# A fused decoder layer: query-phase out-products later, the state's wait for one turned half, another value order, and silu written back into its bank

## The reference, cut to what matters

```
qkv = silu(x @ qkv_w.T)                 # 2 x 512 tokens, 32 heads of 128; q, k, v per head
per block: scores = (q @ k.T) * decay;  intra = scores @ v
           inter  = (q * q_decay) @ state;  state = state * block_decay + (k * k_decay).T @ v
out  = intra + inter
out  = rms_norm(out) * norm_w
out  = sigmoid(x @ gate_w.T) * out
x    = layernorm(x + out @ out_w.T)
```

## Time and profile before

| | |
|---|---|
| runs, median (lowest to highest) | 1945.45 us (1941.33 to 1946.73), three runs |
| profiled execution | 1941.43 us, span 1939.6 us |
| TensorE busy | 93% of the span |
| VectorE / ScalarE / GpSimd busy | 71% / 50% / 33% |
| mean granted TensorE clock | 0.976 |

### The profile page before, as it was taken

One profiled execution on the slowest core, in us unless ns is written; L12 is line 12 of the kernel. 1 busy time (PEld: TensorE's weight loads), 2 busy tenths in 40 slices (PEclk: granted clock), 3 DMA queues, 4 the chain that ended last, 5 costly groups with the idle time before them and its releaser, 6 DMA issues.

```text
span 1939.6 us, 27666 instructions
## 1 busy us (share of the span) xinstructions
PE 1808.5 (93%) x9865; PEld 896.1 (46%) x9865; DVE 1383.3 (71%) x1867; ACT 975.0 (50%) x1432; POOL 641.9 (33%) x506
## 2 busy tenths in 40 slices
PE   6999999999999999999999999999999999999887
PEld 4454535444454534444453544444453544575432
DVE  8677677676777767777766767667676766758877
ACT  5554545544464544545454544545444454544674
POOL 2352323324342333334232332434233332301333
PEclk9999999999999999999999999999999999999998
DMA  4213214231422223041321313131221413233332
GB/s 180 67 66 105 86 66 103 67 103 44 129 62 95 74 87 104 31 133 50 115 76 37 101 55 84 42 102 57 66 71 55 104 46 87 80 100 118 109 88 88
DMA packets 158118, 161.53 MB, mean 83 GB/s; under 512 B 99872, under 2 KB 127904, under 8 KB 157600
## 3 DMA queue, kind: packets, MB, share of 16 engines
q1 hardware_dynamic: 146528, 147.09, 25.6%
q0 software_dynamic: 2560, 8.39, 1.3%
q10 hardware_dynamic: 8896, 4.28, 0.8%
HBM read 123.56 MB, written 12.58 MB: 70 GB/s over the span
## 4 chain that ended last, share of the span: by engine, by line
PE 54%; DVE 17%; issue 16%; ACT 9%; POOL 3%; DMA 1%; ACTq 0%; DVEq 0%; POOLq 0%; SPq 0%
PE bank L1386 13%; PE bank L1387 13%; PE bank L1388 13%; DVE w_pair L1740 4%; PE bank L1359 4%; PE bank L1473 3%; PE bank L1475 3%; PE bank L1474 2%; DVE acc L1908 2%; POOL ssq L2052 1%; ACT sig L1636 1%; DVE gated_split L1740 1%; ACT k_units L1643 1%; ACT w_pair L1601 1%; PE bank L1537 1%
## 5 line engine op out<-in xcount | busy, mean ns | idle before, releaser
L1386 PE MATMUL bank<-x_blocks,w_pair 128*128 128x512 f16 (+1 forms) x1820 | 687.9, 378 | 23.8 <-DVE bank L1788 12.1
L1387 PE MATMUL bank<-x_blocks,w_pair 128*128 128x512 f16 (+1 forms) x1820 | 686.6, 377 | 0.0
L1388 PE MATMUL bank<-x_blocks,w_pair 128*128 128x512 f16 (+1 forms) x1820 | 685.5, 377 | 0.0
L2026 POOL TENSOR_TENSOR sums_pair<-raw_pair 128x512 f32<-128x512 f32 x63 | 93.5, 1485 | 647.8 <-DVE w_pair L1740 453.5
L1386 PEld LDWEIGHTS bank<-x_blocks,w_pair 128*128 128x128 f16 x1820 | 180.1, 99 | 237.4 <-DVE bank L1788 20.1
L1388 PEld LDWEIGHTS bank<-x_blocks,w_pair 128*128 128x128 f16 x1820 | 179.9, 99 | 208.8 <-issue 10.4
L1387 PEld LDWEIGHTS bank<-x_blocks,w_pair 128*128 128x128 f16 x1820 | 180.2, 99 | 195.4 <-issue 12.0
L1908 DVE TENSOR_TENSOR acc<-acc,bank 128x512 f32<-128x512 f32 x320 | 212.0, 681 | 43.6 <-PE bank L1475 41.9
L1473 PE MATMUL bank<-w_vo,gated_split 128*128 128x512 f16 x392 | 150.8, 385 | 57.2 <-issue 54.5
L1636 ACT ACTIVATE sig<-bank 128x512 f32<-128x512 f32 x145 | 86.4, 596 | 227.0 <-PE bank L1388 192.1
L1740 DVE SCALAR_TENSOR_TENSOR w_pair<-raw_pair,w_pair 128x1024 f16<-128x1024 f32 x126 | 170.2, 1370 | 14.0 <-ACT w_pair L1601 13.9
(11 more groups left out here) (208 smaller groups left out, 2792.4 us busy)
## 6 DMA issues: line engine op xcount, KB each, us to landing
raw_pair<-w_qk SPq DMA_DIRECT2D x32, 1024.0 KB, 5.5
raw_pair<-w_gate SPq DMA_DIRECT2D x16, 1024.0 KB, 4.9
raw_pair<-w_out SPq DMA_DIRECT2D x16, 1024.0 KB, 4.9
raw_pair<-w_vt SPq DMA_DIRECT2D x15, 1024.0 KB, 4.9
raw_pair<-ctx_in SPq DMA_DIRECT2D x8, 1024.0 KB, 4.9
decay_sb<-rates SPq DMA_DIRECT2D x60, 128.0 KB, 4.5
acc<-x_t SPq DMA_DIRECT2D x4, 1024.0 KB, 11.5
ctx<-raw_pair SPq DMA_DIRECT2D x8, 512.0 KB, 3.2
```

What stands on the lines that cost most here:

```text
L1386: pe.matmul(out, w_hi, x_hi, start=unmet and k == 0, stop=False, skip_group_check=halves or not fresh)
L1387: pe.matmul(out, w_hi, x_lo, start=False, stop=False, skip_group_check=halves or not fresh)
L1388: mm = pe.matmul(out, w_lo, x_hi, start=False, stop=k == QT - 1, skip_group_check=halves or not fresh)
L2026: pool.tensor_tensor(s3, a11, a21, ALU.add)
```

## The change

Four edits. In the query pair the out stages 0 to 2, and the splits and sums that feed them, move one or two products later, and weight splits 0 and 1 of the next pair move from product 6 to products 5 and 4. The value pair's order becomes 1, 7, 6, 2, 4, 5, 3. The state product waits for the turned even unit alone (`v_first`), not for both of its head's units. And silu writes its result back to where it read it (bank or `p7_copy`), so the `sig` tiles are no longer needed for it; the place is released when the low half is written (for k's units 0 and 2, when the decay multiplication has read it) instead of after the silu.

```diff
 def qk_out(self, which, r):
     done, place, sign = self.result(r)
-    gi, silu, lo = self.silu(...)
-    self.release(place, silu)
-    if which == "k" and r % 2 == 0:
-        self.kd[r // 2] = gi, lo
+    silu, lo = self.silu(...)
+    if which == "k" and r % 2 == 0:
+        self.kd[r // 2] = place, silu
+    else:
+        self.release(place, lo)
...
 def decay_keys(self, g):
-    gi, lo = self.kd[g]
-    self.add("k_decay", g=g, gi=gi, lo=lo, rate=self.rate_ready[g])
+    place, silu = self.kd[g]
+    gi = self.sig_at % 2
+    self.sig_at += 1
+    self.add("k_decay", g=g, gi=gi, place=place, silu=silu, sig_free=self.sig_free[gi], rate=self.rate_ready[g])
     rate = self.rate_free[g] = self.sig_free[gi] = self.tick("k_rate")
+    self.release(place, rate)
...
 # state: what it waits for
-    v=[t for b in range(B) for t in self.v_done[b][g]]
+    v=self.v_first[g]
...
 # kv_out, v_out and end_v
-    self.release(place, silu)
+    self.release(place, lo)
...
+    self.v_first = [[self.v_turned[2]], [self.v_turned[0]]]
...
 # the query pair's slots, order (1, 2, 7, 6, 5, 4, 3) as before
     "p1": [attend(3), gated(3)] + gate_rest,
-    "p2": sums(S2) + stages(0) + [lambda: plan.qk_out("q", 0)] + units(3) + split_sum(S2) + sums(S1),
-    "p7": stages(1) + split_sum(S1) + sums(S4) + split_sum(S4),
-    "p6": stages(2) + [part(0), part(1)],
+    "p2": sums(S2) + [lambda: plan.qk_out("q", 0)] + units(3),
+    "p7": split_sum(S2) + sums(S1) + stages(0) + sums(S4),
+    "p6": split_sum(S1) + stages(1) + split_sum(S4),
+    "p5": stages(2) + [part(0)],
+    "p4": [part(1)],
     "p3": stages(3) + [part(2)],
...
 # the value pair
-}, (1, 7, 6, 4, 2, 5, 3))
+}, (1, 7, 6, 2, 4, 5, 3))
...
 # ScalarE, silu
-    until(act, sem, st["sig_free"])
-    act.activation(c.sig32[st["gi"]][:, :], c.placed(st["place"]), ACT.Silu, ...)
-    src = c.sig32[st["gi"]][:, :]
+    src = c.placed(st["place"])
+    act.activation(src, src, ACT.Silu, ...)
...
 # VectorE, silu's low half and the decay
-    src = c.sig32[st["gi"]][:, :]
+    src = c.placed(st["place"])
...
-    dve.wait_ge(sem["qkv_lo"], st["lo"][1])
+    dve.wait_ge(sem["silu"], st["silu"][1])
+    until(dve, sem, st["sig_free"])
     until(dve, sem, st["rate"])
-    dve.tensor_tensor(k, k, c.rate(st["g"], B), ALU.mult)
+    dve.tensor_tensor(k, src, c.rate(st["g"], B), ALU.mult)
```

More of the change, by code:

```diff
@@ L329, in silu @@
     def silu(self, done, place, sign, dst, dst_free):
[L331 to L333 removed]
+        st = self.add("silu", done=done, place=place, sign=sign, silu=self.tick("silu"),
                       dst=dst, free=dst_free if isinstance(dst_free, list) else [dst_free], slot=self.late_slot,
                       hi=self.tick("qkv_hi"))
[L336 to L337 removed]
+        return st["silu"], self.tick("qkv_lo")
     def qk_out(self, which, r):
         done, place, sign = self.result(r)
[L341 to L343 removed]
+        silu, lo = self.silu(done, place, sign, (which, r), [self.qk_free, self.g_split] if which == "k" else
+                             [self.qk_free, self.q_read])
         if which == "k" and r % 2 == 0:
[L345 removed]
+            self.kd[r // 2] = place, silu
+        else:
+            self.release(place, lo)
         for b in range(B):
@@ L366, in state @@
         i, bank, free = self.main_ring.take()
-        self.add("state", g=g, bank=bank, free=free, turned=self.k_turned[g], v=[t for b in range(B) for t in self.v_done[b][g]],
+        self.add("state", g=g, bank=bank, free=free, turned=self.k_turned[g], v=self.v_first[g],
                  mm=self.tick("state_mm"), hi=self.tick("st_hi"))
@@ L374, in kv_out @@
         done, place, sign = self.result(r)
-        _, silu, lo = self.silu(done, place, sign, ("kv", b, r), [self.qk_free, self.g_split, self.late_units_free])
-        self.release(place, silu)
+        silu, lo = self.silu(done, place, sign, ("kv", b, r), [self.qk_free, self.g_split, self.late_units_free])
+        self.release(place, lo)
         self.qk_done[("k", r // 2, b)] = lo
@@ L385, in v_out @@
         done, place, sign = self.result(r)
-        _, silu, lo = self.silu(done, place, sign, ("v_unit", r), self.s_free if r == 2 else self.vo_free)
-        self.release(place, silu)
+        silu, lo = self.silu(done, place, sign, ("v_unit", r), self.s_free if r == 2 else self.vo_free)
+        self.release(place, lo)
         self.add("v_turn", r=r, ready=lo, free=max(self.v_hl_free))
@@ L420, in end_v @@
         bank = v["banks"][half]
-        _, silu, done = self.silu(v["mm"][half], bank, 1.0, ("v", v["b"], half), self.v_hl_free[v["b"]])
+        silu, done = self.silu(v["mm"][half], bank, 1.0, ("v", v["b"], half), self.v_hl_free[v["b"]])
         self.v_done[v["b"]] = [[done]] * GH
-        self.main_ring.give(bank, silu)
+        self.v_first = [[done]] * GH
+        self.main_ring.give(bank, done)
     def values(self, b):
@@ L1633, in scalar_program @@
         elif kind == "silu":
+            src = c.placed(st["place"])
             act.wait_ge(sem[st["done"][0]], st["done"][1])
-            until(act, sem, st["sig_free"])
-            act.activation(c.sig32[st["gi"]][:, :], c.placed(st["place"]), ACT.Silu,
-                           scale=st["sign"] / W_SCALE).then_inc(sem["silu"])
-            src = c.sig32[st["gi"]][:, :]
+            act.activation(src, src, ACT.Silu, scale=st["sign"] / W_SCALE).then_inc(sem["silu"])
             act.wait_ge(sem["silu"], st["silu"][1])
```

4 lines of the change are left out of this document (2 added, 2 removed).

## The result

| | before | after |
|---|---|---|
| median (lowest to highest), four runs each, same job | 1945.39 us (1941.33 to 1946.73) | 1863.7 us (1861.19 to 1864.07) |
| profiled execution | 1941.43 us, span 1939.6 us | 1863.91 us, span 1862.1 us |
| mean granted TensorE clock | 0.976 | 0.992 |

The ratio is 0.9581 (95% interval 0.9564 to 0.9597).

A forecast was written before the change was run, and what follows sets the result against it. TensorE was taken as the bound, busy 1808.5 of 1939.6 us. Terms −65.5 − 13.6 + 9.2 + 0.6 = −69.3 us took the profiled 1941.43 to 1872.1; 4.0 more for the median gave 1876 us, range 1866 to 1901.

The forecast's parts named there:

- the term for silu in its bank: Value pair and first key pair: same instructions and shapes, but a new wait at bank 2, +9.2 and +0.6 us.
- the state, put at nothing: State matmuls, waiting for one turned half: no wait listed ahead of them, so 0 us; any gain would be small.
- the 4.0 us added to get from a profile to a median: Whole kernel: the median of three runs, 1945.45 us, lay 4.0 above the profiled 1941.43, so 1872.1 became 1876.2.
- Query stages, −65.5 forecast: Query pair: later out stages save 4.83 us in each of 13 stages and 2.7 in the first, −65.5 us.
- Rival (c): Query pair: gated block S2 still ends last, now ahead of stage 1; 11 to 28 us more, chance 0.12.
- rival (b): Query stages: the clock still falls after the 1.71 us wait; 24 to 41 us more, chance 0.08.
- The hold at bank 2, +9.2 forecast: Value pair: product 7 waits 0.66 us for the decay multiplication to free bank 2, 14 times, +9.2 us.
- Rival (a): Value pair: bank 2 costs as much as today's queue allows, 2.6 us per group; 27 us more, chance 0.12.
- The value order, −13.6 forecast: Value pair: product 2 ahead of product 4 covers the wait for U3, 0.97 us in each of 14, −13.6 us.
- Value stages, −4.4 forecast: Value stages: the value order's −13.6 us and the bank 2 wait's +9.2 us taken together, −4.4 us.
- Ahead of the loop, +0.6 forecast: First key pair, ahead of the repeated stages: the new bank 2 wait occurs once more, +0.6 us.
- the 0.065 us more for a bank source: VectorE's one low half in the bank 2 path: 62 more cycles for a PSUM source, 0.9 us in all.

The follow-up runs named there:

- the kernel with the decay and the gate first: Kernel after, with the decay multiplication ahead of the weight split and unit 2's gate sigmoid (bank 2) ahead of unit 3's: 1851.38 us, ratio 0.9521.

## Why the prediction was right, and where it failed

The large step was right: the later out stages take away the long wait and with it the low clock. Three steps failed. The first is the term for silu in its bank, costed as "same instructions, same shapes" with its waits alone: VectorE's busy time in a value stage fell from 17.55 to 14.47 us, which removed a hidden wait ahead of out stage 14 (0.2 us a group, about 2.5 us in all) and made the value order's term one that two edits share. The second is the state, put at nothing because the list shows no wait there: it gave 2.7 us. The third is the 4.0 us added to get from a profile to a median: it measured −0.2. Against 1876.2 the median is 12.5 us lower: 8.2 on the profiled execution (1872.1 against 1863.91) and 4.2 between the executions.

**Query stages, −65.5 forecast, −66.4 measured.** Right in size and in its steps. A later stage lasts 26.54 us (26.6 forecast) and the first 24.79 (24.9). TensorE's timeline of the kernel after shows product 2's end, product 7's start behind 1.72 us (1.71 forecast), stage 1's two products and product 5:

```profile
548.76 0.38 PE L1393 MATMUL bank<-x_blocks,w_pair 128*128 128x512 f16 x1
...
550.85 0.39 PE L1391 MATMUL bank<-x_blocks,w_pair 128*128 128x512 f16 x1 [1.72 <-ACT gate_units L1632]
...
557.34 0.38 PE L1478 MATMUL bank<-w_vo,gated_split 128*128 128x512 f16 x1
...
557.99 0.38 PE L1478 MATMUL bank<-w_vo,gated_split 128*128 128x512 f16 x1
...
558.63 0.38 PE L1391 MATMUL bank<-x_blocks,w_pair 128*128 128x512 f16 x1
```

From 557.34 to 558.63 are six matmuls at 0.215 us: S2, asked at 557.99, was ready. The two gated splits end at 553.96 + 2.46 = 556.42, 5.6 us after product 7 starts, as forecast (579.3 against 573.74); in the earlier trace rows it was 7.2 us. Rival (c) did not come here; with stage 0 moved back it did, and cost 0.9 us of idle time. The full gain needs silu's bank form as well, which keeps query silu's low half short: without it the stage lasts 27.2 (the query order alone, and the kernel with the `sig` tiles), and product 5 waits for U3.

**The clock.** All 14 query stages have 1.00, so rival (b) did not come either. But the reason given against it was weak. The prediction took a wait of 3.48 us with full clock behind it as a sign that a shorter one does no harm. In the kernel with silu in its bank alone, every query stage has a fall: the first behind a wait of 3.00 us, the later ones behind waits of 3.48 us. The window behind the one shown above:

```profile
576.90:580.30 3.40, 3.40 (x10) 1.21 (x9) 2.18 (x3) 0.00 (x0) 1.03 (x1) 0.51 0.00 0
```

So it was luck that the reasoning from that one case came out. That waits of 1.72 us leave the 2.4 GHz level as it is, only the kernels with the new query order show.

**The hold at bank 2, +9.2 forecast.** Right: 0.61 us from start to start in the kernel after, and 8.5 us in the medians when the multiplication goes first. Product 7 could have started at 600.67 − 0.61 = 600.06; the split began 1.5 us before that (1.4 forecast) and ended 1.09 us after GpSimd's addition (1.1 forecast), and the multiplication was through at 600.61. Rival (a), with 2.6 us, did not come.

**The value order, −13.6 forecast.** The 0.97 us a group are right for the edit alone (24.81 to 23.81 us), but the prediction booked them to an edit that is worth nothing once silu writes in its bank (24.26 and 24.27 us). Both edits remove the same wait for U3, one by asking later and one by letting VectorE reach its addition sooner, 6.69 instead of 8.20 us after the start of product 7. How much of the latter is VectorE's shorter work and how much the hold at bank 2 was not separated. The prediction had noted that the stretched k halves go, but used that for the hold at bank 2 alone. The sum was still near by luck, because only one of the two edits was counted.

**Value stages, −4.4 forecast, −7.6 measured.** 0.7 us of the 3.2 is the hold (0.05 × 14). The other 2.5 are a second wait that the list of waits doesn't have: ahead of out stage 14, TensorE waited for VectorE's accumulation, which ended at 632.78 + 1.28 = 634.06. Timeline of TensorE before, last matmul of product 6 and the first of stage 14, then last matmul of the value pair and the first of the state:

```profile
633.70 0.38 PE L1388 MATMUL bank<-x_blocks,w_pair 128*128 128x512 f16 x1
634.12 0.39 PE L1473 MATMUL bank<-w_vo,gated_split 128*128 128x512 f16 x1
...
650.78 0.38 PE L1388 MATMUL bank<-x_blocks,w_pair 128*128 128x512 f16 x1
651.19 0.33 PE L1359 MATMUL bank<-v_split,scores_keys 128*128 128x128 f16 x3
```

And the same four places in the timeline after:

```profile
606.94 0.38 PE L1393 MATMUL bank<-x_blocks,w_pair 128*128 128x512 f16 x1
607.15 0.38 PE L1478 MATMUL bank<-w_vo,gated_split 128*128 128x512 f16 x1
...
622.82 0.38 PE L1393 MATMUL bank<-x_blocks,w_pair 128*128 128x512 f16 x1
623.04 0.33 PE L1364 MATMUL bank<-v_split,scores_keys 128*128 128x128 f16 x3
```

The steps from row to row are 0.42 and 0.41 before, 0.21 and 0.22 after; the pitch is 0.216. Since a record is 0.38 us long, a wait of up to 0.16 us leaves no gap and a wait of 0.2 us one of 0.03 or 0.04: the row has no bracket and the list no entry. The prediction knew of the overlap and added it to the waits it had, but took an absent entry for no wait. Stage 14's wait goes with the bank form: 23.81 with the value order alone, 23.83 with the `sig` tiles, 23.65 with bank form and the decay first.

**State, 0 forecast, −2.7 measured.** The same error: about 0.2 us in each of the 13 gate stages behind a value stage. The single edit gave 2.7 us in the gate stages and a median ratio of 0.9984.

**Ahead of the loop, +0.6 forecast, −1.0 measured.** The list has no wait for the decay multiplication there, so the term for the first key pair did not come. One wait got shorter: TensorE's single wait for C22 (`p_copy`) is 1.4 us in the list after, and it was 2.4 in the list of before. The prediction didn't weigh it.

**From the profiled execution to the median, +4.0 forecast, −0.2 measured.** The prediction added the 4.0 us by which the median of three runs of before stood above its profiled run. Over the 33 runs of before beside the experiments the median is 1943.77 us, only 2.3 above it, so part of the 4.0 was the chance of three runs. The falls of the clock have a share in before's scatter: the five of those runs with a mean granted clock of 0.973 or 0.974 took 1945.63 to 1948.55 us, the other 28 took 1940.79 to 1946.87. (In the query stages half clock came to 64.9 us in the profile of before, 51.2 in those of the value order alone and of silu in its bank alone.) But the eight kernels above without falls in the query stages scatter as well, by 1.1 to 4.6 us over five runs, and the profiled run of the one with stage 0 back stands 3.3 us above its median (1861.47 against 1858.17). So the −0.2 is luck too, and what moves these runs is not shown. The prediction held the case "the profile's run as the typical one (−4)" for its low end alone.

## What to carry to other kernels

An edit that only changes where an operand lies also changes how long its neighbours' instructions last; cost the queue of that engine anew before costing any other edit that waits for it, for two edits may remove the same wait, as the value order and the bank did here. Where records overlap, compare the distance from start to start with the pitch at each place where the change takes a wait away: a wait shorter than the overlap has no entry in any list, one of 0.2 us hardly shows, and 13 of these are 2.7 us. Do not add the offset between one profiled run and a median of three as if it were a term of its own: here it was 4.0 us for three runs and 2.3 for 33.

## What the hardware showed that was not expected

**Source in a bank against source in SBUF.** On VectorE the low half of 128x512 takes 0.69 us from a bank, beside GpSimd or not, and 1.35 us from the `sig` tile beside a GpSimd addition. With no GpSimd addition beside it, v's low half takes a median of 0.693 us from the `sig` tile (before) and 0.692 from the bank (after); the 0.065 us more for a bank source, which the prediction weighed as an estimate, is not there. The same goes the other way: GpSimd's addition of 512 columns takes 1.27 us while VectorE reads a bank, and 2.13 us across a weight split. That VectorE with two SBUF inputs and GpSimd exclude each other is what the Trainium skill says in "SBUF — State Buffer", section "SBUF: two separate sides"; these rows agree.

**The clock.** TensorE kept its 2.4 GHz level in every query stage of the kernel after, with one wait of 1.72 us in each of the 13 later ones; in the kernel before it fell to 1.2 GHz after the waits of 3.9 us. After waits of 3.48 us it did both: it stayed up in the first stage of before and fell in 13 stages of the kernel with silu in its bank alone. In the kernel with the decay and the gate first, TensorE's busy time in the query stages is the same 24.4 us as after, so no clock was left to win.
